# The first LSTM window length inside a graph loop: rows made straight from PSUM, two gates kept in PSUM, and another order of loads and reflections

## What is computed

```
h = relu(einsum('ts,bsh->bth', adj, x @ Wg0 + bg0))
h = relu(einsum('ts,bsh->bth', adj, h @ Wg1 + bg1))
for p in 1..4:                       # windows of p nodes, zero initial state
    g = x_t @ Wih[p-1].T + h_state @ Whh[p-1].T + bias     # gates i, f, g, o
    c = sigmoid(f) * c + sigmoid(i) * tanh(g);  h_state = sigmoid(o) * tanh(c)
    rows p-1, 2p-1, ... of h = last h_state of each window
```

## Time and profile before

| | |
|---|---|
| median of 3 runs | 2043.29 us (2043.22 to 2044.27) |
| the profiled execution | 2044.89 us |
| its span, first to last instruction | 2043.1 us |
| granted TensorE clock, mean over the span | 0.971 of full speed |
| busy: PE, DVE, ACT, POOL | 1915.3 (94%), 1519.5 (74%), 1152.8 (56%), 712.2 (35%) us |

### The profile page before, as it was taken

How to read it: one execution, slowest core, us unless ns; L and a number is a source line. 1 busy time by engine, 2 the same in 40 slices (tenths; PEclk the granted TensorE clock), 3 DMA queues, 4 the chain that set the end, 5 groups by cost and what they waited for, 6 DMA issues and landing times. The chain is left out here.

```text
span 2043.1 us, 32231 instructions
## 1 busy us (share of the span) xinstructions
PE 1915.3 (94%) x11545; PEld 1616.9 (79%) x11545; DVE 1519.5 (74%) x4011; ACT 1152.8 (56%) x1803; POOL 712.2 (35%) x1676
## 2 busy tenths in 40 slices
PE   6999999999999999999999989989699899689996
PEld 5888887888899999987887778867599434479895
DVE  6888786657566777888888879868565588789575
ACT  3555556445445454544344367657576688557575
POOL 2566651233233341000000056466543000108675
PEclk8999999999999999999999989989799999899898
DMA  3010101001000000010000043113212000003022
GB/s 115 22 32 22 52 1 42 1 1 42 1 1 1 1 1 1 1 42 1 1 1 1 1 150 104 63 38 97 73 65 71 1 1 1 11 30 128 22 73 83
DMA packets 61534, 71.13 MB, mean 35 GB/s; under 512 B 3767, under 2 KB 55102, under 8 KB 61374
## 3 DMA queue, kind: packets, MB, share of 16 engines
q1 hardware_dynamic: 61374, 69.07, 10.4%
HBM read 43.90 MB, written 25.17 MB: 34 GB/s over the span
## 5 line engine op out<-in xcount | busy, mean ns | idle before, releaser
L2002 ACT ACTIVATE l_gates<-l_acc,l_b 128x512 f32<-128x512 f32 (+1 forms) x408 | 240.7, 620 | 88.3 <-PE l_acc L475 86.3
L1900 ACT ACTIVATE l_x_hi<-hT 128x512 fp32r<-128x512 f32 (+1 forms) x144 | 101.2, 754 | 171.4 <-PE l_acc L475 170.9
L473 PE MATMUL l_acc<-l_x_hi,l_w1x_hi 128*128 128x336 f32 (+1 forms) x544 | 187.9, 345 | 4.0 <-ACT l_gates L2002 2.7
L475 PE MATMUL l_acc<-l_x_lo,l_w1x_hi 128*128 128x336 f32 (+1 forms) x544 | 188.3, 346 | 0.0
L474 PE MATMUL l_acc<-l_x_hi,l_w1x_lo 128*128 128x336 f32 (+1 forms) x544 | 188.3, 346 | 0.0
L473 PE MATMUL l_acc<-l_x_hi,l_w0x_hi 128*128 128x512 f32 x464 | 182.2, 393 | 5.4 <-ACT l_gates L2002 4.5
L475 PE MATMUL l_acc<-l_x_lo,l_w0x_hi 128*128 128x512 f32 x464 | 181.5, 391 | 0.0
L474 PE MATMUL l_acc<-l_x_hi,l_w0x_lo 128*128 128x512 f32 x464 | 181.3, 391 | 0.0
L2009 ACT ACTIVATE l_gates<-l_cell 128x512 f32<-128x512 f32 (+1 forms) x112 | 63.8, 569 | 191.2 <-DVE l_cell L2061 155.7
L244 POOL TENSOR_TENSOR bi_shifted<-bi_shifted 32x126 f32<-32x126 f32 (+61 forms) x62 | 17.7, 286 | 378.2 <-DVE bi_shifted L231 378.2
L1247 ACT ACTIVATE leaky<-sc_g 128x1024 f32<-128x1024 f32 x128 | 121.2, 1032 | 21.7 <-PE sc_g L1361 21.4
(11 more groups left out here) (519 smaller groups left out, 6231.3 us busy)
## 6 DMA issues: line engine op xcount, KB each, us to landing
xin<-in_x_t SPq DMA_DIRECT2D x16, 512.0 KB, 3.7
hidB<-in_x SPq DMA_DIRECT2D x16, 512.0 KB, 4.8
x<-hT SPq DMA_DIRECT2D x16, 512.0 KB, 3.2
hidB<-x SPq DMA_DIRECT2D x16, 512.0 KB, 3.8
x<-hidB SPq DMA_DIRECT2D x16, 512.0 KB, 2.9
attention_residual<-x SPq DMA_DIRECT2D x16, 512.0 KB, 3.9
out_x<-hT SPq DMA_DIRECT2D x16, 512.0 KB, 2.9
l_rawx<-in_wih SPq DMA_DIRECT2D x4, 1024.0 KB, 5.4
```

The costliest lines, as they stand in the source:

```text
L473: t.matmul(out, left[0], right[0], start=start, stop=False)
L475: return t.matmul(out, left[0], right[1], start=False, stop=stop)
L1900: i = nc.scalar.activation(as_windows(xs[s % 2][0][:, ch, 0:bg * nw], nw), cols(p, bg, nw, group, k, ch), ACT.Copy)
L2002: i = a.activation(gates[:, j, q, 0:n], acc[:, j, q, 0:n], FUNC[q], bias=b[:, o:o + 1])
```

## The change

- `rows_out` is gone. `rows_high` for p = 1 makes `l_x_hi` by one Relu from `ps_out` (128 x 1024), `rows_low` makes `l_x_lo` by one instruction from `ps_out` and `l_x_hi`. What waited for `rows_out` now waits for `l_x_lo`.
- Gate g and the tanh of the cell are written back into their PSUM bank of the ring; DVE reads them there. A bank is free once the cell or the product into `hT` has been made, and the waits of the LSTM products say so.
- `y` of group 2 lies in pair c too; the waits of `project_input(2)` and `mix_to_features(1)` follow.
- Reflections: none at (2, 1); that of turn 2 stands behind `rows_low` on DVE; that of turn 16 moves to its second half. 28 are in the loop, so the later stages do one more.
- The first graph weights are loaded second, the second ones after the biases; ACT waits for each alone, and the first projection waits for the low part of the weights, and for the bias only before its first bias matmul.
- The first products of window length 2 no longer wait for the last gate of length 1: only its second half does, for `hT`.

```diff
-REFLECTION_AT = {at: k for k, at in enumerate([(it, half) for it in range(2, 16) for half in range(2)] + [(16, 0)])}
+REFLECTION_AT = {at: k for k, at in enumerate([(2, 0)] + [(it, half) for it in range(3, 16) for half in range(2)] + [(16, 1)])}
...
-            return as_rows(pair_c if g == 1 else pair_a)
+            return as_rows(pair_c if g in (1, 2) else pair_a)
...
             sp.dma_start(xin[0][:, :, :], xv[0]).then_inc(x_in, 16)
+            sp.dma_start(raw[:, 0], wg0.rearrange("(c p) n -> p c n", p=P)).then_inc(w0_in, 16)
...
-            sp.dma_start(raw[:, 0], wg0.rearrange("(c p) n -> p c n", p=P)).then_inc(w_in, 16)
-            sp.dma_start(raw[:, 1], wg1.rearrange("(c p) n -> p c n", p=P)).then_inc(w_in, 16)
...
             sp.dma_start(b1r[64:65, :], bg1).then_inc(b_in, 16)
+            sp.dma_start(raw[:, 1], wg1.rearrange("(c p) n -> p c n", p=P)).then_inc(w1_in, 16)
...
-            act.wait_ge(w_in, 32)
+            act.wait_ge(w0_in, 16)
...
+            act.wait_ge(w1_in, 16)
             a.activation(w1[0][:, :, :], raw[:, 1], ACT.Copy).then_inc(hi_w, 1)
...
-                    rows_out(early)
                     lstm.rows_high(act, early)
...
-                reflection((it, 0))
+                if it > 2:
+                    reflection((it, 0))
...
                     lstm.rows_low(dve, early)
+                if it == 2:
+                    reflection((it, 0))
...
-                if g >= 2:
+                if g >= 3:
                     pe.wait_ge(axl, g - 1)
+                elif g == 2:
+                    pe.wait_ge(yl, 2)
                 if g == 0:
-                    pe.wait_ge(lo_w, 2)
+                    pe.wait_ge(lo_w, 1)
...
+                    if g == 0 and r == 0:
+                        pe.wait_ge(lo_w, 2)
...
-                    pe.wait_ge(out, g - 1)
+                    pe.wait_ge(lstm.rows_ready, g - 1)
...
-                if 1 <= g < GROUPS - 1:
+                if 2 <= g < GROUPS - 1:
                     pe.wait_ge(yl, g + 2)
...
-                if p == 2:
-                    pe.wait_ge(rows_done, GROUPS)
-                    pe.wait_ge(ring_read, 6 * GROUPS)
...
+                        elif step + k == GROUPS:
+                            pe.wait_ge(hd, 2 * GROUPS)
...
+                if p == 1:
+                    act.wait_ge(layer_done, group + 1)
+                    nc.scalar.activation(xs[s % 2][0][:, :, :], layer_out, ACT.Relu).then_inc(x_hi, 1)
+                    return
...
+                if p == 1:
+                    nc.vector.scalar_tensor_tensor(lo[:, :, :], layer_out, 0.0, hi[:, :, :].bitcast(F32), ALU.max,
+                                                   ALU.subtract).then_inc(x_lo, 1)
+                    return
...
-                    pe.wait_ge(ring_read, n - RING + 1)
+                    half, kind = divmod(n - RING, 3)
+                    if kind == 0:
+                        pe.wait_ge(ring_read, n - RING + 1)
+                    else:
+                        pe.wait_ge((cl, hd)[kind - 1], half + 1)
...
+                to = ring(group, j, m) if q == 2 else gates[:, j, q]
+                nc.scalar.activation(to, ring(group, j, m), FUNC[q], bias=b[:, o:o + 1]).then_inc(ring_read, 1)
...
+            act.wait_ge(ring_read, 6 * group + 3 * j + 3)
             act.wait_ge(cl, 2 * group + j + 1)
-            nc.scalar.activation(tcell[:, j], cell[:, j], TANH).then_inc(tc, 1)
+            nc.scalar.activation(ring(group, j, 2), cell[:, j], TANH).then_inc(tc, 1)
...
-            nc.vector.tensor_tensor(cell[:, j], gates[:, j, 0], gates[:, j, 2], ALU.mult).then_inc(cl, 1)
+            nc.vector.tensor_tensor(cell[:, j], gates[:, j, 0], ring(group, j, 1), ALU.mult).then_inc(cl, 1)
...
-            o3, t3 = (as_windows(z, nw) for z in (gates[:, j, 3], tcell[:, j]))
+            o3, t3 = (as_windows(z, nw) for z in (gates[:, j, 3], ring(group, j, 2)))
```

More of the change, by code:

```diff
@@ L1413, in ps_y @@
         def ps_y(g):
-            return as_rows(pair_c if g == 1 else pair_a)
+            return as_rows(pair_c if g in (1, 2) else pair_a)
         ps_h1, ps_ax, ps_out = as_rows(pair_b), pair_a, pair_b
         ps_sums = acc[:, 1, 0, 0:P]
-        w_in, x_in, b_in = sem("g_w_in"), sem("g_x_in"), sem("g_b_in")
+        w0_in, w1_in, x_in, b_in = sem("g_w0_in"), sem("g_w1_in"), sem("g_x_in"), sem("g_b_in")
         l_in, l_hi, l_lo = sem("g_l_in"), sem("g_l_hi"), sem("g_l_lo")
         hi_w, lo_w, sums, sums_done, cleared = sem("g_w_hi"), sem("g_w_lo"), sem("g_sums"), sem("g_sums_done"), sem("g_cleared")
-        xh, xl, p1, yh, yl, m1, h1h, h1l, m2, axh, axl, p2, out = (sem("g_" + n) for n in (
-            "x_hi", "x_lo", "project1", "y_hi", "y_lo", "mix1", "h1_hi", "h1_lo", "mix2", "ax_hi", "ax_lo", "project2", "hT"))
+        xh, xl, p1, yh, yl, m1, h1h, h1l, m2, axh, axl, p2 = (sem("g_" + n) for n in (
+            "x_hi", "x_lo", "project1", "y_hi", "y_lo", "mix1", "h1_hi", "h1_lo", "mix2", "ax_hi", "ax_lo", "project2"))
         off, loaded, adj_loaded, ones_set, ident_zero, ident_set = (sem("const_" + n) for n in (
@@ L1687, in project_output @@
                 else:
-                    pe.wait_ge(out, g)
+                    pe.wait_ge(lstm.rows_ready, g)
                 if g == 0:
@@ L1712, in on_tensor @@
                     lstm.products(pe, early, 0)
-        return (on_sync, on_gpsimd, on_scalar, on_vector, on_tensor), (out, l_lo, (p1, m1))
+        return (on_sync, on_gpsimd, on_scalar, on_vector, on_tensor), (ps_out, p2, l_lo, (p1, m1))
 class FirstWindows:
@@ L1722, in __init__, with lstm_layers @@
             "products", "gates", "tanh", "cell", "hidden"))
-        self.rows_high, self.rows_low, self.weights_high, self.weights_low = (parts[n] for n in (
-            "rows_high", "rows_low", "weights_high", "weights_low"))
-def lstm_layers(nc, sem, c, hT, acc, wih, whh, first_weights, bi, hh, rows_done, first_done, graph_done):
+        self.rows_high, self.rows_low, self.weights_high, self.weights_low, self.rows_ready = (parts[n] for n in (
+            "rows_high", "rows_low", "weights_high", "weights_low", "rows_ready"))
+def lstm_layers(nc, sem, c, hT, acc, wih, whh, first_weights, bi, hh, layer_out, layer_done, first_done, graph_done):
     with ExitStack() as ctx:
@@ L1960, in first_gates @@
                 o = 2 * q + j
-                i = nc.scalar.activation(gates[:, j, q], ring(group, j, m), FUNC[q], bias=b[:, o:o + 1])
-                i.then_inc(ring_read, 1)
+                to = ring(group, j, m) if q == 2 else gates[:, j, q]
+                nc.scalar.activation(to, ring(group, j, m), FUNC[q], bias=b[:, o:o + 1]).then_inc(ring_read, 1)
         def first_tanh(act, group, j):
+            act.wait_ge(ring_read, 6 * group + 3 * j + 3)
             act.wait_ge(cl, 2 * group + j + 1)
-            nc.scalar.activation(tcell[:, j], cell[:, j], TANH).then_inc(tc, 1)
+            nc.scalar.activation(ring(group, j, 2), cell[:, j], TANH).then_inc(tc, 1)
         def first_cell(dve, group, j):
             dve.wait_ge(ring_read, 6 * group + 3 * j + 2)
-            nc.vector.tensor_tensor(cell[:, j], gates[:, j, 0], gates[:, j, 2], ALU.mult).then_inc(cl, 1)
+            nc.vector.tensor_tensor(cell[:, j], gates[:, j, 0], ring(group, j, 1), ALU.mult).then_inc(cl, 1)
         def first_hidden(dve, group, j):
@@ L2089, in lstm_layers @@
         first = FirstWindows(products=first_products, gates=first_gates, tanh=first_tanh, cell=first_cell, hidden=first_hidden,
-                             rows_high=rows_high, rows_low=rows_low, weights_high=weights_high, weights_low=weights_low)
+                             rows_high=rows_high, rows_low=rows_low, weights_high=weights_high, weights_low=weights_low, rows_ready=x_lo)
         return (on_sync, on_gpsimd, on_scalar, on_vector, on_tensor), first, signals
@@ L2101, in first_layers @@
         acc = early.enter_context(nc.psum_tensor("l_acc", [P, C, 4, GROUP], F32))
-        graph, (rows_done, first_done, graph_done) = graph_layers(
+        graph, (layer_out, layer_done, first_done, graph_done) = graph_layers(
             nc, sem, c, hT, acc, a["x_t"], a["adj"], a["adj_t"], a["wg0"], a["bg0"], a["wg1"], a["bg1"], bi, hh, a["wih"], a["bias"], lw)
-        lstm, first, signals = lstm_layers(nc, sem, c, hT, acc, a["wih"], a["whh"], lw, bi, hh, rows_done, first_done, graph_done)
+        lstm, first, signals = lstm_layers(nc, sem, c, hT, acc, a["wih"], a["whh"], lw, bi, hh, layer_out, layer_done, first_done, graph_done)
     m = edge_indices(wide, nc)
```

2 lines of the change are left out of this document (removed).

## The result

| | before | changed |
|---|---|---|
| median of 4 runs each | 2043.26 us | 2024.04 us (2021.84, 2023.38, 2024.70, 2026.28) |
| profiled execution | 2044.89 us | 2021.84 us |
| its span | 2043.1 us | 2020.0 us |
| granted clock over the span | 0.971 | 0.973 |
| DVE, ACT, POOL busy | 1519.5, 1152.8, 712.2 us | 1519.1, 1134.7, 659.6 us |

The change saves 19.2 us in the medians and 23.1 us between the two profiled executions. Forecast were 25.2 us and a median of 2018.1, in a range of 2015.5 to 2023.5. The direction and the mechanism of most terms hold; one term that was taken as nothing, part 7, isn't nothing, and 2024.04 lies above the range.

A forecast was written before the change was run, and what follows sets the result against it. The prediction took PE to bound the kernel, with waits for DVE in the graph loop; 1.7 + 1.4 + 10.7 + 7.1 + 4.3 = 25.2 us saved off the median 2043.29 gave 2018.1 us, range 2015.5 to 2023.5.

The forecast's parts named there:

- part 7: Later LSTM stages: one reflection moved there from the loop is covered by DVE's idle time; cost 0, bounds 0 to 1.
- Part 1: Start of the loop: order of loads and split wait let the first projection start earlier; 1.7 us, bounds 0 to 2.2.
- Part 2: Before projecting group 2: with `y` in pair c PE no longer waits for `ax_lo`; 1.4 us, bounds 1.0 to 1.4.
- Part 3: Turn 2: pair c and the later reflection cut it from 25.58 to 14.85 us; 10.7 us, bounds 7 to 10.8.
- part 4: Turns 3 to 14: fewer two-SBUF-input DVE instructions hold POOL, so turns fall to 19.04 us; 7.1 us, bounds 0 to 7.1.
- second rival: Turn 2: a narrow place is missed, PE idles about 3 us and half clock follows; 5 us less saved, 2023.3; chance 0.07.
- first rival: Turns 3 to 14: POOL stays held as before; 18.1 us saved, 2025.2; chance 0.09.
- Parts 5 and 6: Loop: ACT's lighter work and gates in PSUM cost and gain nothing; new waits cost 0, bounds 0 to 3.
- third rival: Each loop turn: `l_x_lo` becomes the bound and PE waits for it; 5 us slower, 2048; chance 0.02.
- Part 8: Loop's end, 310.46 to 344.84: reflection behind `l_x_lo` and no gate wait before the second length; 4.3 us, bounds 2.3 to 4.3.
- my opening: Behind the graph loop, the first 345 us, PE is busy without a gap, so the loop's saving arrives at the end whole.

The follow-up runs named there:

- e9: The changed kernel with `y` of group 2 in pair a again, the reflection of turn 2 as changed: 2025.06 us, ratio 0.9905.
- e11: The changed kernel with one more reflection in window length 2 and that of turn 2 behind `ax_lo` of group 1: 2024.89 us, ratio 0.9905.
- e7: The changed kernel with the reflection of turn 2 ahead of `l_x_lo` again, pair c kept: 2033.16 us, ratio 0.9946.
- e4: The changed kernel with rows through `hT` and gate g and tanh of the cell in SBUF again: 2036.15 us, ratio 0.9962.
- e6: The changed kernel with only the rows through `hT` again, the gates still in PSUM: 2027.45 us, ratio 0.9918.
- e12: The changed kernel with only gate g and tanh of the cell in SBUF again, rows still from PSUM: 2023.94 us, ratio 0.9898.
- e3: The kernel before without its reflection at (16, 0), so 28 in the loop and one more later: 2046.15 us, ratio 1.0007.
- e2: The changed kernel with a 29th reflection back in the loop, at the head of turn 16: 2022.64 us, ratio 0.9895.
- e10: The changed kernel with the extra later reflection in window length 2, first step of its second group: 2025.53 us, ratio 0.9911.

## Why the prediction missed, point by point

- **Part 1 (1.7) held: 1.64.** In the changed kernel ACT begins `wg_hi` at 5.57, and PE waits for its low part, for the earlier trace rows:

```profile
5.57 0.61 ACT L1496 ACTIVATE wg_hi<-g_raw 128x512 fp32r<-128x512 f32 x1
...
6.83 0.69 DVE L1576 TENSOR_TENSOR wg_lo<-g_raw,wg_hi 128x512 fp32r<-128x512 f32 x1
...
7.67 0.55 PE L473 MATMUL l_acc<-wg_hi,xs_hi 128*128 128x256 f32 x1 [0.98 <-DVE wg_lo L1576]
```

- **Part 2 (1.4) was there at first and not whole at the end of turn 2:** 1.2 to 1.5 us in the matmul starts between 27 and 34 us, but 0.7 to 1.0 us over turns 1 and 2 in e9, at or under its lower bound of 1.0.
- **Part 3 (10.7) gave 9.7.** The turn is 15.90 and not 14.85 us. I had counted 4.4 us for the reflection behind `l_x_lo` and nothing in front of it. The trace of the changed kernel shows what I left out:

```profile
30.61 2.32 POOL L189 TENSOR_SCALAR bi_shifted<-bi_shifted 32x1 f32<-32x1 f32 x1 [19.06 <-DVE bi_shifted L180]
...
33.57 1.54 POOL L191 TENSOR_SCALAR bi_shifted<-bi_shifted 32x1 f32<-32x1 f32 x1
```

```profile
36.90 0.15 DVE L206 RECIPROCAL bi_shifted<-bi_shifted 32x1 f32<-32x1 f32 x1 [0.70 <-POOL bi_shifted L196]
...
41.53 1.20 DVE L1567 TENSOR_TENSOR ax_lo<-l_acc,ax_hi 128x1024 fp32r<-128x1024 f32 x1
```

```profile
42.87 0.36 PE L473 MATMUL l_acc<-wg_hi,xs_hi 128*128 128x256 f32 x1 [0.70 <-DVE ax_lo L1567]
```

  L189 takes 0.26 us elsewhere and 2.32 beside the weight split (2.27 us), L191 is the one beside `xs_lo`; both of these have two SBUF inputs, so POOL was held there too. DVE waits 0.70 us for it, and PE waits 0.70 us for `ax_lo`. This is the rule of my own part 4, not applied in part 3. The other 0.35 us are no wait: PE is busy 15.20 us in this turn, where my sum of blocks was 14.85, and e11, without the wait, takes 15.10. It was the second rival at a fraction of its price (1.0 us for 5): a few tenths of idle time left the clock at 1.00, as argued. Of the two edits of turn 2 the prediction gave the credit to pair c; e7 and e9 show that the place of the reflection ends the long wait.
- **Part 4 (7.1) held: 7.08**, on the mechanism named. e4, e6 and e12 show the mechanism. They also show that half the edit isn't needed, since I priced rows and gates together. The first rival is refuted. The Trainium skill, in SBUF — State Buffer, "Who interferes with whom", says that a VectorE instruction with two SBUF inputs contends with a GpSimd instruction that reads SBUF. The runs agree: with three such instructions left in the lagging half (e6) 17.0 of 23.9 us of wait stay, with two (e12) 7.1, with one (changed) 0.5.
- **Parts 5 and 6 held:** no wait of PE for `l_x_lo` or `l_gates` in the loop; the third rival never came near.
- **Part 8 (4.3) held: 4.13.**
- **Part 7, "taken 0, bounds 0 to 1", failed: 2.1 us at the start of the bisection (e3).** This is the step that failed. I said the reflection was covered because DVE is 69% busy beside a full PE. That window, 400 to 500 us, is the wrong stretch. The reflection landed at 777 us, ahead of the bisection, and from there on DVE is 85% busy and with ACT sets the pace. What stands ahead of such a stretch on DVE is paid there although PE is full beside it; "behind it PE is busy without a gap", my opening, isn't so for 812 to 1170 us. e2 shows the same from the other side, 1.8 us, and e10 gives the stage back its 80.71 us. How much of it reaches the end isn't shown: e2 has no better median than the changed kernel.
- **The clock behind a wait of 2.2 us.** At 732.13 the kernel before waits 2.18 us and keeps its clock; at 707.94 the changed one waits 2.19 us and loses it for a while. Windows of 8 us, before:

```profile
732.00:740.00 8.00, 7.36 (x46) 7.08 (x47) 6.35 (x12) 3.33 (x8) 6.56 (x9) 1.00 0.01 2
```

changed:

```profile
708.00:716.00 8.00, 8.00 (x42) 8.00 (x43) 6.34 (x11) 3.26 (x7) 6.38 (x9) 0.79 0.01 2
```

  That is the other 0.5 us of the 2.6 lost there: with the extra reflection the stage takes 82.74 us in e3, which keeps its clock, and 83.28 here. Nine of the twelve traces lose the clock behind this wait; the kernel before, e3 and e10 keep it.
- **From span to median, and the range.** The sum was made between profiled executions, where 23.1 of 25.2 us came. 3.8 more are missing in the medians: the profiled execution before lay 1.6 us above its median, the changed one 2.2 us below. The three runs of before had agreed within 1.1 us, and I took that for the spread; the 15 of the first series of experiments run from 2042.10 to 2045.51. The range carried the bounds of single terms and no spread of executions. With the 2.1 us of part 7 and the 1.0 of part 3 the forecast would have been 2021.2. Of the 2.8 us left, 0.7 is the base (all 36 runs of the kernel before have a median of 2043.96, not 2043.29) and 1.1 is the four runs of the result (2024.04, where all eight have 2022.95); the last 1.0 us is within the 4.4 us that the changed kernel varies by. The traces show where that spread arises. From the last L109 of the bisection to the end, behind everything that was changed, the twelve take 869.7 to 872.7 us; the two of the changed kernel are the shortest (869.7 and 869.9), the kernel before has 870.7. A part of it is the clock behind a wait of 6.0 us, the first 16 us behind it in the changed kernel:

```profile
1319.63:1335.63 16.00, 14.15 (x56) 11.60 (x57) 6.85 (x10) 6.96 (x10) 9.23 (x14) 0.79 0.02 7
```

  and in e9, with six matmuls fewer:

```profile
1318.41:1334.41 16.00, 14.15 (x50) 11.55 (x51) 5.84 (x9) 5.64 (x8) 8.23 (x14) 0.69 0.00 0
```

  That the executions of the changed kernel without a trace lost their time in the same places is likely and not shown.

## What to carry to other kernels

A POOL chain of tiny operations is as slow as the DVE instructions beside it that read two SBUF tensors: give one operand a PSUM home, where it already is, and look for the same pair in every stretch, not only in the one that shows the wait. Work moved off a busy stage is sure to be free only if it lands where its engine has slack until the end: read the busy share of that engine at the place it lands and behind it. And take the spread from more than three executions when a kernel has waits near 2 us on TensorE.

## What the runs showed of the hardware

- One POOL instruction on 32 numbers (L191) took 0.33, 1.50, 2.71 or 3.31 us, by what DVE did beside it (e4, e6, changed). It was held over up to four DVE instructions in a row and ended 0.2 us after the last of them.
- A gate written to PSUM took 0.66 us, to SBUF 0.69 (0.69 too as the mean of all three gates in the kernel before); tanh of the cell 0.60, and 0.63 before. DVE took 1.20 us for 128x1024 from two SBUF tensors and from SBUF and PSUM. The home of these operands changed other engines' times and hardly their own:

```profile
L1973 ACT ACTIVATE l_gates<-l_acc,l_b 128x512 f32<-128x512 f32 x41 | 28.3, 689 | 23.6 <-PE l_acc L475 23.6
L1973 ACT ACTIVATE l_acc<-l_acc,l_b 128x512 f32<-128x512 f32 x21 | 13.9, 663 | 13.5 <-PE l_acc L475 13.5
L1978 ACT ACTIVATE l_acc<-l_cell 128x512 f32<-128x512 f32 x21 | 12.6, 602 | 0.7
```

- After a PE wait of 2.2 to 2.4 us the lower clock followed in some traces and not in others, with the same code around it: 8.92 us (changed) against 7.36 (e12) for the same 35 matmuls and the wait before them. Behind both waits it followed in nine traces of twelve.
